# Ranking moved one turn earlier, the softplus subtraction moved to VectorE, and one more state's input scaled on GpSimd

## What is computed

```python
x = x + attn(_layernorm(x), ...)         # attn: below
x = x + moe(_layernorm(x), ...)

# attn, u is the normed input
xm, z = split(u @ in_proj_w.T)
xc = silu(conv(xm) + conv_b)
dt, Bm, Cm = split(xc @ x_proj_w.T)
dt = softplus(dt @ dt_proj_w.T + dt_proj_b)
h  = h * exp(dt * A) + dt * B * xc       # scan over time, 16 states
y  = (sum over states of h * C) + xc * D_skip
x  = x + (y * silu(z)) @ out_proj_w.T
x  = x + (silu(gate) * a) @ ff_out_w.T   # a, gate = split(norm(x) @ ff_proj_w.T)

# moe
p = softmax(x / norm(x) @ router_w)      # 8 experts
rw, sel = top_k(p, 2); rw = rw / sum(rw)
out = sum over experts e of combine[:, e] * (x @ Wa[e] @ Wb[e])
```

## Time and profile before

| | |
|---|---|
| median of 3 runs | 1366.08 us (1365.59 to 1366.9) |
| profiled execution | 1364.54 us |
| its span in the trace | 1362.8 us |
| mean granted TensorE clock | 0.976 of full speed |
| TensorE matmul busy | 1231.1 us (90%) |
| GpSimd busy | 1092.7 us (80%) |
| ScalarE busy | 1057.8 us (78%) |
| VectorE busy | 971.3 us (71%) |

### The profile page before, as it was taken

The page is one execution under the profiler, slowest core; times in us unless marked ns, Lnnn a source line. Parts: engine busy times, 40 slices in busy tenths (PEclk is TensorE's granted clock), DMA queues, the critical chain, the costliest instruction groups (busy, mean ns, idle before and its releaser), DMA issues.

```text
span 1362.8 us, 24300 instructions
## 1 busy us (share of the span) xinstructions
PE 1231.1 (90%) x7680; PEld 1058.5 (78%) x7680; DVE 971.3 (71%) x1765; ACT 1057.8 (78%) x2537; POOL 1092.7 (80%) x826
## 2 busy tenths in 40 slices
PE   4587889999999999999999999999999999898986
PEld 3366777887878787787878878787887878787875
DVE  2486868778786876878687786868778686878621
ACT  3798898888787878878788887878788787878420
POOL 3389798888888888888888888888888888788721
PEclk8798899999999999999999999999999999999998
DMA  1411102111121111112111111211121021202001
GB/s 65 171 47 40 39 26 77 40 47 63 48 79 46 57 40 56 56 48 79 49 56 40 66 46 48 79 48 56 40 79 47 33 71 48 71 24 73 30 32 47
DMA packets 29223, 75.08 MB, mean 55 GB/s; under 512 B 3104, under 2 KB 15776, under 8 KB 26528
## 3 DMA queue, kind: packets, MB, share of 16 engines
q1 hardware_dynamic: 29088, 73.41, 16.1%
HBM read 64.61 MB, written 4.59 MB: 51 GB/s over the span
## 4 chain that ended last, share of the span: by engine, by line
PE 72%; ACT 9%; DVE 7%; issue 5%; POOL 2%; DMA 0%; DVEq 0%; ACTq 0%; POOLq 0%; SPq 0%
PE psx L1185 12%; PE psy L1204 12%; PE psb L1062 8%; PE psb L1068 8%; PE pst L1068 8%; PE pst L1062 6%; DVE h L976 3%; ACT dA L801 2%; PE psf L1062 2%; ACT bxT L789 2%; PE psf L1153 2%; PE psf L1159 2%; PE psf L1094 2%; PE psb L1159 2%; PE psf L1105 2%
## 5 line engine op out<-in xcount | busy, mean ns | idle before, releaser
L976 DVE TENSOR_TENSOR_SCAN h<-dA,state,psx 128x256 f32<-128x256 f32 x1024 | 681.4, 726 | 112.8 <-PE psx L1185 99.2
L575 POOL TENSOR_TENSOR hC<-h,bC 128x1024 f32<-128x1024 f32 x256 | 606.1, 2372 | 96.0 <-DVE h L976 73.8
L801 ACT ACTIVATE dA<-dt,neg_a 128x256 f32<-128x256 f32 x1024 | 434.3, 500 | 0.0
L1185 PE MATMUL psx<-ident,bxT 128*128 128x128 f32 x2048 | 307.0, 276 | 25.2 <-DVE h L976 15.2
L789 ACT ACTIVATE bxT<-uTs,BT 128x512 f32<-128x512 f32 x384 | 254.1, 717 | 67.4 <-PE psx L1185 65.8
L1185 PEld LDWEIGHTS psx<-ident,bxT 128*128 128x128 f32 x2048 | 246.2, 143 | 68.5 <-issue 24.3
L1204 PE MATMUL psy<-ident,hC 128*128 128x128 f32 x2048 | 267.6, 274 | 1.5 <-POOL hC L575 1.5
L1204 PEld LDWEIGHTS psy<-ident,hC 128*128 128x128 f32 x2048 | 235.2, 143 | 4.5 <-POOL hC L575 1.7
L559 POOL TENSOR_TENSOR bxT<-uTs,BT 128x1024 f32<-128x1024 f32 x64 | 121.5, 1898 | 32.0 <-PE psx L1185 32.0
L1062 PE MATMUL psb<-nT,w_ff_sb 128*128 128x256 f32 x496 | 121.8, 388 | 12.9 <-ACT yg L814 11.7
L1062 PE MATMUL pst<-eT,w_a_sb 128*128 128x256 f32 x448 | 107.2, 382 | 14.2 <-DVE cbc L1032 14.2
(11 more groups left out here) (148 smaller groups left out, 1633.7 us busy)
## 6 DMA issues: line engine op xcount, KB each, us to landing
bC<-bc_scratch SPq DMA_DIRECT2D x64, 512.0 KB, 3.8
cbc<-cw_scratch SPq DMA_DIRECT2D x16, 1024.0 KB, 4.7
xf<-in_x SPq DMA_DIRECT2D x16, 256.0 KB, 2.7
xk<-xn SPq DMA_DIRECT2D x16, 256.0 KB, 4.3
xb<-in_x SPq DMA_DIRECT2D x16, 256.0 KB, 4.2
out<-x SPq DMA_DIRECT2D x16, 256.0 KB, 2.2
w_in_sb<-in_w_in SPq DMA_DIRECT2D x1, 1024.0 KB, 5.2
w_ff_sb<-in_w_ff SPq DMA_DIRECT2D x1, 1024.0 KB, 5.9
```

Of the source, the lines that this page charges most:

```text
L575: nc.gpsimd.tensor_tensor(hC[:, s % RC], h[:, ring(s)], bC[:, g % RINGG, s % G:s % G + 1, :].to_broadcast([P, NJ, T]), ALU.mult).then_inc( ...
L801: last = nc.scalar.activation(dA[:, s % RA, j, :], dt[:, n[1], j, :], ACT.Exp, scale=neg_a[:, j, s:s + 1])
L976: last = nc.vector.tensor_tensor_scan(h[:, r, j, :], dA[:, s % RA, j, :], psx[bx_bank(fill)][:, k, :], state[:, b, j, s:s + 1], ALU.mult, ...
L1185: last = nc.tensor.transpose(psx[bx_bank(fill)][:, k, j * P:(j + 1) * P], bxT[:, ring(s), j, c:c + P], ident[:, :])
```

## The change

`POOL_STATES` gets state 6 as well. The exponential `pr` and the ranking move from turn 3 to turn 2. ScalarE's order of stages becomes `back, ready, enter, tail` in turn 2 and `back, tail, ready, enter` in turn 4; in the other turns `tail` stays first. The subtraction of the softplus leaves GpSimd's turn 8 and becomes a `tensor_tensor` of VectorE in turn 9, behind `tail`'s work of that turn.

```diff
-POOL_STATES = (4, 8, 14, 15)
+POOL_STATES = (4, 6, 8, 14, 15)
...
             def ready(s, m):
                 b = m[1]
-                if s == 8:
-
-                    pool.wait_ge(sp_fix, count(1, m, 1))
-                    nc.gpsimd.tensor_tensor(sp_l[:, :, :], sp_l[:, :, :], sp_e[:, :, :], ALU.subtract
-                                            ).then_inc(sp_rest, 1)
                 if s == 9:
...
-                if s == 3:
+                if s == 2:
...
-                if s == 3:
+                if s == 2:
                     act.wait_ge(lgm_done, count(1, m, 1))
                     nc.scalar.activation(pr[:, :, :], lgm[:, :, :], ACT.Exp).then_inc(pr_done, 1)
...
-            drive(act, {"else": ("tail", "back", "ready", "enter")}, enter, ready, main, back, tail)
+            drive(act, {2: ("back", "ready", "enter", "tail"), 4: ("back", "tail", "ready", "enter"),
+                        "else": ("tail", "back", "ready", "enter")}, enter, ready, main, back, tail)
...
+                if s == 9:
+                    dve.wait_ge(sp_fix, count(1, m, 1))
+                    nc.vector.tensor_tensor(sp_l[:, :, :], sp_l[:, :, :], sp_e[:, :, :], ALU.subtract).then_inc(sp_rest, 1)
```

## The result

| | before | changed |
|---|---|---|
| median | 1366.49 us (4 runs, 1365.59 to 1368.71) | 1345.57 us (4 runs, 1340.51 to 1349.1) |
| ratio to before | | 0.9842, 95% interval 0.9807 to 0.9876 |
| profiled execution, its span | 1364.54 us, 1362.8 us | 1344.57 us, 1342.8 us |
| granted TensorE clock | 0.976 | 0.982 |

The change wins 20.9 us. The forecast was 25.8 us won and 1340.

The account below looks back on a forecast made before the run. TensorE was taken as the bound, waiting for ScalarE's copy `yg`. Shorter `yg` waits 23.7, opening 1.1 and clock 1.0 sum to 25.8 us won, bringing the median from 1366.08 to 1340 (1334 to 1346, chance 0.60).

Parts of the forecast that it names:

- steady 16.5, less the 0.04 each: TensorE's wait for `yg` before the output projection, eleven steady iterations: 16.5 us, less 0.04 each, so 16.0 won.
- It just fits: Second half of `x`: VectorE's six taps end at 618.8, TensorE comes at 618.85; 0.04 us each allowed.
- GpSimd is just in time: GpSimd's queue after ranking and `bxT` 6: ready for product 6 at 627.2, needed at 627.4; costed at nothing.
- The subtraction: Softplus subtraction on VectorE: 1.8 us in the loop at cost 0 (bounds 0 to +0.7), 1.2 in the opening.
- the sentence on SyncE: Sync queue: later product 3 holds the load of `bC` by under 1 us, ahead of `cw`'s store; cost nothing.
- the forecast of 3.9 and 2.0: Two last iterations, copy `yg` seen earlier by TensorE: 2.5 us plus clock up to 1.4, and 2.0 won.
- The opening and the first copy: Subtraction shortened beside idle GpSimd, 1.1 us; first copy of `yg`, at 146.72, without ScalarE's `bxT`, 1.2 us won.
- The closing: Last part of the run, with its own order, the same in effect: 0 won.
- The clock: Eight TensorE matmuls after the longest waits stay at 2.4 GHz: up to 2.0 us back, 1.0 taken.
- (a): Subtraction's delay reaches TensorE through the gate: some 0.8 us in 14 iterations, 1351; with milder mixes with (b), chance 0.23.
- (b): VectorE stays late at the taps; TensorE waits at `x`'s second half, the 16.0 are lost: 1356; whole, chance 0.04.
- (c): Ranking starts late on GpSimd because `pr` comes at 610.64: about 1.3 us lost in 13 iterations, 1381; chance 0.08.

Follow-up runs that it names:

- Experiment 4: Changed kernel with the load of `bC` issued two turns later, behind `cw`'s store and `cbc`'s load: 1339.14 us, ratio 0.9807.
- experiment 9: Kernel before with the load of `bC` group 2 issued in turn 6 instead of turn 4: 1364.45 us, ratio 0.9998.
- experiment 12: Changed kernel measured again, unaltered: 1344.02 us.
- experiment 2: Kernel before with only the softplus subtraction moved to VectorE's turn 9: 1363.31 us, ratio 0.9986.
- experiment 6: Changed kernel with the softplus subtraction back on GpSimd in turn 8: 1345.82 us, ratio 0.986.
- experiment 7: Kernel before with state 6's input on GpSimd and ScalarE's new order in turn 4, ranking left in turn 3: 1394.31 us, ratio 1.0203.
- experiment 3: Kernel before with only state 6's input moved to GpSimd, ranking still in turn 3: 1402.47 us, ratio 1.0271.
- experiment 1: Kernel before with only the ranking and its exponential in turn 2 and ScalarE's new order: 1357.61 us, ratio 0.9947.
- experiment 8: Kernel before with the load of `bC` group 2 held until `cT` and issued right before `cw`'s store: 1370.5 us, ratio 1.0027.
- experiment 10: Changed kernel with the late `bC` load, second group of hidden values in `psb`, VectorE's last taps ahead of its first `cbc` product: 1337.53 us, ratio 0.9804.

## Why the prediction was right, and where it was wrong

**The chain was read rightly.** ScalarE's input of state 6 and `cw` stood between TensorE and the copy `yg`. The sum of "steady 16.5, less the 0.04 each" gives 1.45 per iteration, and ten of eleven show 1.47 on average. "It just fits" held twice: the copy and the six taps come with no idle time of TensorE at 606.30 and 610.21. The ranking begins at 598.48. VectorE's `lgm`, two instructions ahead of it on the chain, starts at 597.45 here and at 606.14 before, 8.69 apart, so on the clock of before that is 607.17; the forecast was 607.1. "GpSimd is just in time" held too: its product 6 starts at 618.78 after an idle 0.44, where 2.38 stood before.

**The subtraction** took 1.74 to 1.92 in the steady iterations (once 1.24) and 1.23 in the opening, against 1.8 and 1.2; the reading of line 960, that it stands still while GpSimd works, carried over to it. In this iteration it takes 1.90: it starts at 630.63 while GpSimd's product 8 runs from 629.09 to 631.45, and ends 1.08 after it:

```profile
629.09 2.36 POOL L570 TENSOR_TENSOR hC<-h,bC 128x1024 f32<-128x1024 f32 x1 [3.21 <-DVE h L975]
...
632.68 2.37 POOL L542 TENSOR_TENSOR dt<-dt,sp_l 128x1024 f32<-128x1024 f32 x1 [1.23 <-DVE sp_l L962]
```

**The step that failed** is the sentence on SyncE: "Product 3, at 618.2, holds a load of `bC` on the sync queue by under 1 us; ... and `cw`'s store behind it needs `cT` at 619.5 anyway. I cost all this at nothing." I asked when the store would be issued. That was right in the steady iterations and wrong in the two last, where the load holds it for 0.9 us. And I didn't ask what it would find in the DMA engines: half a megabyte just in front of it, on a path (store, its landing, load, its landing) with some 9 us of room in a steady iteration and 5.5 in the two last. With a slow landing on top it cost 3.0 in one steady iteration, and with the 0.9 us on the queue the whole of the 2.0 of the last one: without TensorE's waits of 1.83 and 2.47 at 1160.78 and 1232.72 these two would have won 3.9 and 2.2, near the forecast of 3.9 and 2.0. Experiment 4 takes the step away, and the time is 1339.1, where the forecast was 1340; its mean period is 77.52, where 77.5 was forecast.

The Trainium skill has the rule on its page "DMA: Bandwidth & Descriptors", section "Two DMAs through the same engine are not ordered": within one queue of a DMA engine descriptors start in order. The gaps here agree (1.3 with the load 3.3 us ahead, 2.5 to 2.8 with it 0.4 to 0.5 ahead, each without a packet of queue 14 beside the store). They don't tell that order from mere sharing of the engines: no run puts the two transfers on different queues. The same sentence of the prediction would have been a cost had I held that rule against it.

**Terms of the wrong size.** The opening and the first copy were taken at 2.3 and won 4.6: the subtraction's 1.2 is there (`xc` of the second step at 48.14 instead of 49.16, from a start 0.17 later), and the rest comes between 49 and 177, with no single row that carries it. It is no more than single executions differ by there: the row at 172.93 stands at 174.35 in the second trace of the same changed kernel, and the one at 177.55 at 175.15 in experiment 9, which changes only the place of one load. So that the terms came out near the forecast in sum is in part luck. The closing was taken at 0 and lost 1.1. Its order of work is the same. TensorE waits there for `cw`, in both kernels, and in both falls to the lower clock once:

```profile
1283.76 0.58 PE L1297 MATMUL pst<-ident,cw 128*8 128x128 f32 x2 [3.06 <-ACT cw L873]
1284.14 3.15 PE L1067 MATMUL psb<-w_out_sb,yg 128*128 128x256 f32 x8
```

In before, the slow eight matmuls were those ahead of that wait (3.67 at 1299.84, and then only 1.38 of waiting), so they cost nothing; here they are the ones behind it, 3.15 instead of 1.89. The clock, put at 1.0 won, gave back what was expected at 220 and 1170, where the eight matmuls take 1.99 now, and took 1.5 at 385 and 1.3 at 1284, each behind a long wait. It took 1.7 more at 194.44, where eight matmuls took 3.57 (granted clock 0.53) behind waits of 1.44 and 0.56; the same waits left them at 1.89 in before and in experiment 12. It lies in the stretch to 253.23, which won 1.57 where 2.6 was forecast.

**The rivals.** (a) didn't come, and experiments 2 and 6 bound it at nothing. (b) is real, and experiment 7 shows it at 2.1 us an iteration, but the early ranking keeps it away. (c) was priced at 1381 for a ranking that is late by 1.9 us; experiments 3 and 7 have such a ranking, for another reason, and cost 36 and 29.

## What to carry to other kernels

An instruction moved between queues has no price of its own: state 6 on GpSimd cost 36 us alone and brought 12 behind the earlier ranking, so price a change with several parts in their combination, and ask of each which wait it makes shorter that another part would make longer. Where a product comes later, follow what it releases down to the DMAs, and for each small transfer on a path ask which large one goes just in front of it, whether that one can hold it on the issuing queue, and how long the whole round trip may be. A wait that a trace shows as a fixed 1.2 us in each of 12 iterations need not be worth 14: look first how much idle time the engine has that is waited for.

## What the runs showed of the hardware

- **A 512 KB load in front of an 8 KB store delays its landing.** Where no `instruction` packet runs beside the store, the gap is 1.29 to 1.35 with the load 2.8 us or more ahead, 1.61 to 2.00 with it 1.4 us ahead, and 2.47 to 2.83 with it 0.4 to 0.5 ahead.
- **`instruction` packets coincide with the other slow transfers.** With one of queue 14 beside the store the gaps are 1.40 to 3.34 without the load in front, 2.46 to 2.99 with it 1.4 ahead and 3.11 to 3.85 with it 0.4 to 0.5 ahead. One of queue 8 often costs nothing, but the largest gaps of the changed kernel (3.70 and 4.01, the load 1.4 ahead) have one beside them. `cbc`'s load lands in 4.2 to 6.0 us as a rule; in all eight cases of 6.2 to 7.6 a packet of queue 8 began within 0.5 us of its issue. That they are the cause is not shown.
- **Longer waits can cost twice.** Counted over all traces between 180 and 1270 us, eight matmuls of 128x256 directly behind a wait of TensorE: behind waits of up to 1.6 us none of some 400 took longer than 1.99, behind waits of 1.7 to 2.9 us 15 of 34 did (2.57 to 3.67), behind waits of 3.06 us and more all 15 (3.21 to 3.68). Between 1.7 and 2.9 the wait's length does not tell: after 1.90 they took 3.14 once and 1.99 once in experiment 1.
- **The opening is not the same in each execution.** TensorE's matmuls into `psf` from `w_dt_sb`, where the clock rises from its lower to its upper level, of the kernel before and of experiment 2:

```profile
27.19 1.10 PE L1153 MATMUL psf<-low,w_dt_sb 128*128 128x256 f32 x4 [0.56 <-ACT low L722]
```

```profile
26.96 2.05 PE L1151 MATMUL psf<-low,w_dt_sb 128*128 128x256 f32 x4 [0.57 <-ACT low L717]
```

The granted clock from 27 to 29 us is 1.00 in the first and 0.50 in the second. Four of the fourteen profiled executions had 2.05 there (experiments 1, 2, 8 and 10), and in those the third step's `xc` started at 105.5 to 107.25 instead of 102.6 to 104.2, whatever the edit. The kernel before spreads over 1361 to 1370 us in all its runs. So 3 us between two single profiles of this kernel are no finding. The Trainium skill's page "TensorE: Matmul & The Clock Gate", section "What's actually happening", says that the number of matmuls at the lower level at the start differs from run to run; the two rows agree.
